# Two attention ends: odd sequences' exact scores in two banks more, normalised input turned in another bank, half of the perceptron's first layer ahead of the last weighing

## The reference

```python
# second attention layer (and, with other weights and no gate, the fifth)
qc = (_ln(x) @ cq_W) per head;  kc, vc = (cond_tokens @ ck_W, @ cv_W) per head   # 77 keys
x  = x + g_x * (softmax(qc @ kc.T / sqrt(8), masked) @ vc) @ co_W
# the perceptron behind it
xm = _ln(x) * (1 + sc_mlp) + sh_mlp
x  = x + g_mlp * (gelu(xm @ mlp_W1 + mlp_b1) @ mlp_W2 + mlp_b2)
```

## Time and profile before

| | us |
|---|---|
| median of 3 runs | 1077.26 (1077.23 to 1077.37) |
| profiled execution, its own time | 1078.58 |
| its span, first to last instruction | 1076.8 |
| TensorE busy in it | 1024.1 (95%) |
| VectorE / GpSimd / ScalarE busy | 780.5 / 681.1 / 593.2 |
| mean granted TensorE clock | 0.978 |

### The profile page before, as it was taken

One profiled execution on the slowest core, in us unless ns is written; L12 is line 12 of the kernel. 1 busy time (PEld: TensorE's weight loads), 2 busy tenths in 40 slices (PEclk: granted clock), 3 DMA queues, 4 the chain that ended last, 5 costly groups with the idle time before them and its releaser, 6 DMA issues.

```text
span 1076.8 us, 28749 instructions
## 1 busy us (share of the span) xinstructions
PE 1024.1 (95%) x11713; PEld 643.3 (60%) x11713; DVE 780.5 (72%) x1940; ACT 593.2 (55%) x842; POOL 681.1 (63%) x783
## 2 busy tenths in 40 slices
PE   7899999999998999999999699999999999999898
PEld 5345555666654776667766455665655566565476
DVE  7889888788874444777777979888888766777321
ACT  2144444577666454555444266665666667765652
POOL 6688887688974432111214689987888766788520
PEclk9699999999999999999999789999999999999999
DMA  6200000000000102000000000000000000000011
GB/s 218 112 2 3 21 12 12 23 12 22 21 12 24 39 29 101 7 6 7 7 7 18 13 7 2 2 2 2 2 2 2 2 2 2 2 2 2 2 39 40
DMA packets 9282, 22.76 MB, mean 21 GB/s; under 512 B 1392, under 2 KB 1648, under 8 KB 8768
## 3 DMA queue, kind: packets, MB, share of 16 engines
q1 hardware_dynamic: 9152, 20.94, 5.8%
HBM read 18.77 MB, written 2.15 MB: 19 GB/s over the span
## 4 chain that ended last, share of the span: by engine, by line
PE 82%; DVE 8%; issue 4%; ACT 3%; POOL 2%; DMA 0%; SPq 0%; DVEq 0%; POOLq 0%; ACTq 0%
PE weighed L674 12%; PE scores L647 11%; PE row_scores L616 8%; PE scores L861 6%; PE weighed L697 5%; PE quads L552 4%; PE scores L571 4%; DVE negmax L1171 3%; PE quads L578 3%; PE row_scores L861 3%; PE quads L563 3%; PE scores L659 3%; PE scores L687 2%; ACT p L1662 2%; PE weighed L872 2%
## 5 line engine op out<-in xcount | busy, mean ns | idle before, releaser
L1171 DVE TENSOR_REDUCE negmax<-row_scores 128x8 f32<-128x616 f32 (+1 forms) x312 | 298.9, 958 | 86.1 <-PE row_scores L616 67.4
L1662 ACT ACTIVATE p<-scores 128x1024 f32<-128x1024 f32 (+1 forms) x256 | 247.6, 1018 | 156.6 <-PE scores L659 156.3
L647 PE MATMUL scores<-qblk,work 32*77 32x512 f32 (+1 forms) x1280 | 203.7, 612 | 10.2 <-ACT p L1662 6.8
L1840 POOL TENSOR_TENSOR kblk_r<-work,pack_const 128x308 fp32r<-128x308 f32 (+1 forms) x160 | 133.6, 836 | 75.3 <-PE row_scores L616 55.4
L674 PE MATMUL weighed<-p,v 77*32 77x128 f32 (+1 forms) x5120 | 173.1, 276 | 2.5 <-DVE nat L1196 2.5
L1830 POOL TENSOR_TENSOR qblk<-work,pack_const 128x512 f32<-128x512 f32 x160 | 166.0, 1038 | 0.9 <-PE scores L647 0.9
L616 PE MATMUL row_scores<-kblk_r,qr 32*128 32x308 f32 (+1 forms) x624 | 142.3, 447 | 18.4 <-DVE negmax L1171 17.3
L674 PEld LDWEIGHTS weighed<-p,v 77*32 77x32 f32 (+1 forms) x5120 | 130.1, 109 | 37.9 <-issue 33.5
L616 PEld LDWEIGHTS row_scores<-kblk_r,qr 32*128 32x128 f32 x624 | 62.0, 187 | 120.0 <-issue 84.5
L1877 POOL TENSOR_TENSOR attn<-nat,rden 128x128 f32<-128x128 f32 x160 | 65.6, 410 | 57.8 <-DVE rden L1201 56.9
L1196 DVE STREAM_TRANSPOSE nat<-weighed 128x256 f32<-128x256 f32 x160 | 70.8, 442 | 34.2 <-PE weighed L674 33.8
(11 more groups left out here) (309 smaller groups left out, 1850.3 us busy)
## 6 DMA issues: line engine op xcount, KB each, us to landing
shared<-gates_hbm SPq DMA_DIRECT2D x24, 256.0 KB, 3.2
shared<-in_ctx_tok SPq DMA_DIRECT2D x15, 154.0 KB
pack_w_l<-in_w_l SPq DMA_DIRECT2D x1, 2058.5 KB, 11.3
x<-in_x_tok SPq DMA_DIRECT2D x8, 256.0 KB, 5.8
out_x<-x SPq DMA_DIRECT2D x8, 256.0 KB, 2.0
layers_w<-in_w_l SPq DMA_DIRECT2D x1, 1289.0 KB, 9.4
ctxT<-in_ctxT SPq DMA_DIRECT2D x1, 1232.0 KB, 9.4
layers_w<-in_w_ada SPq DMA_DIRECT2D x1, 582.0 KB, 5.1
```

Source lines behind the costliest of these rows:

```text
L647: mm = e.matmul(scores[0:nk, g, :], k_of[q % 3][at, s * nk:(s + 1) * nk], qblk[n % 2][at, :], start=layer.mask != "qk", stop=False, skip_g ...
L1171: e.tensor_reduce(negmax[q % 2][:, 2 * h:2 * h + 2, s * NJ:(s + 1) * NJ], row_banks(n, h)[:, :, 0:NJ * nk].rearrange("p g (j k) -> p g j k ...
L1662: e.activation(p[n % 2][0:nk, 8 * h:8 * h + 8, :], scores[0:nk, 2 * h:2 * h + 2, :].rearrange("p g (j q) -> p (g j) q", j=NJ), ACT.Exp, bi ...
L1840: e.tensor_tensor(kblk_r[n % 2][:, 0:NJ * nk].rearrange("p (j k) -> p j k", j=NJ), k_of[q % 3][:, s * nk:(s + 1) * nk].unsqueeze(1).to_bro ...
```

## The change

In the last five slots of each phase the exact scores of an odd sequence (59, 61, 63 and 155, 157, 159) put their second half, groups 2 and 3, in the two banks of `row_scores`, whose row maxima are all taken by then; their Exp reads it there. Even sequences stay in the four banks of `scores`. With that, `exact` in these slots waits for `exp_done >= 2n - 1`, the first half of the sequence before, and for all row maxima. `shift` is called once per half. The perceptron's norms of slots 59, 63 and 155, 159 are turned in the quads' bank (`quad_bank`), and no wait of `exact` stands behind them. `first_layer` of the first quad is split: its chunks 0 and 1 (banks 2 and 3 of `scores`) stand ahead of the last `weigh`, chunks 2 and 3 (`row_scores`) behind it. `project_out` in slots 62 and 158 drops its wait for an Exp.

```diff
+        def turned_in_quads(it):
+
+
+            return not it.family or 0 < 4 * PHASES[it.q >= 2 * NB][1] - it.slot <= 5
+
         def turned_bank(it):
-
-            return scores[:, 1, :] if it.family else quad_bank[:, :]
+            return quad_bank[:, :] if turned_in_quads(it) else scores[:, 1, :]
...
             return any(4 * lo <= n < 4 * lo + 4 for lo, _ in PHASES)
+
+        def from_end(n):
+
+            return min(4 * hi - n for _, hi in PHASES if n < 4 * hi)
+
+        def score_banks(n, h):
+
+
+            return row_scores[:, :, :] if h and n % 2 and from_end(n) <= 5 else scores[:, 2 * h:2 * h + 2, :]
...
                 layer, nk = layer_of(q), layer_of(q).nk
-                w.wait_ge(exp_done, 2 * n)
+                if from_end(n) <= 5:
+                    w.wait_ge(exp_done, 2 * n - 1)
+                    w.wait_ge(max_done, 2 * (n + from_end(n)))
+                else:
+                    w.wait_ge(exp_done, 2 * n)
                 ready, value = k_ready(q)
...
                     at = slice(TILE * g, TILE * (g + 1))
-                    mm = e.matmul(scores[0:nk, g, :], k_of[q % 3][at, s * nk:(s + 1) * nk], qblk[n % 2][at, :],
+                    mm = e.matmul(score_banks(n, g // 2)[0:nk, g % 2, :], k_of[q % 3][at, s * nk:(s + 1) * nk], qblk[n % 2][at, :],
                                   start=layer.mask != "qk", stop=False, skip_group_check=True,
...
-            def shift(n):
+            def shift(n, h):
                 q, s = divmod(n, QUAD)
...
                 w.wait_ge(act_setup, ACT_AT["select"])
-                for g in range(NG):
-                    at = slice(TILE * g, TILE * (g + 1))
-                    mm = e.matmul(scores[0:nk, g, :], select[at, s, 0:nk], nblk[q % 2][at, :], start=False, stop=True,
-                                  skip_group_check=True, tile_position=(TILE * g, 0))
-                    if g % 2:
-                        mm.then_inc(shifted, 1)
+                for i in range(2):
+                    at = slice(TILE * (2 * h + i), TILE * (2 * h + i + 1))
+                    mm = e.matmul(score_banks(n, h)[0:nk, i, :], select[at, s, 0:nk], nblk[q % 2][at, :], start=False, stop=True,
+                                  skip_group_check=True, tile_position=(TILE * (2 * h + i), 0))
+                mm.then_inc(shifted, 1)
...
-            def first_layer(phase, c, hi):
+            def first_layer(phase, c, hi, chunks=range(4)):
                 weight, in_done, act_done = (("l0_w1", mlp_in, mlp_act), ("l3_w1", ffn_in, ffn_act))[phase]
...
                 w.wait_ge(max_done, 8 * hi)
-                w.wait_ge(exp_done, 8 * hi)
+                w.wait_ge(exp_done, 8 * hi - (2 if chunks.stop == 2 else 0))
                 w.wait_ge(ln_done, NORM_OF[("l0m", "l3f")[phase], hi - NB + c].index + 1)
-                for f in range(4):
+                for f in chunks:
                     w.wait_ge(act_done, 4 * (c - 1) + f + 1)
...
                     qi, cl = divmod(t, QUAD)
-                    if t in norm_at and norm_at[t].family:
+                    if t in norm_at and not turned_in_quads(norm_at[t]):
                         w.wait_ge(ln_scaled, norm_at[t].index + 1)
...
                         w.wait_ge(raw_done, (qi + 3) % NB + 1)
-                    if t in norm_at and not norm_at[t].family:
+                    if t in norm_at and turned_in_quads(norm_at[t]):
                         w.wait_ge(ln_scaled, norm_at[t].index + 1)
...
                         turn_x(qi + 3)
-                    if t in norm_at and not norm_at[t].family:
+                    if t in norm_at and turned_in_quads(norm_at[t]):
                         turn_normed(norm_at[t])
                     if cl == 2 and qi - 2 in quads and not is_wide(t):
-                        w.wait_ge(exp_done, early)
+                        if qi >= hi:
+                            w.wait_ge(exp_done, early)
                         project_out(qi - 2)
...
                         exact(t)
-                        shift(t)
+                        shift(t, 0)
+                        shift(t, 1)
                     if is_wide(t):
...
                     else:
+                        if t == 4 * hi:
+                            first_layer(phase, 0, hi, range(2))
                         if t - 1 in jobs:
...
                         keep_busy(5, scores[:, 0, 0:128])
-                    if first_layer_at(t, hi) is not None:
-                        first_layer(phase, first_layer_at(t, hi), hi)
+                    c = first_layer_at(t, hi)
+                    if c is not None:
+                        first_layer(phase, c, hi, range(0 if c else 2, 4))
                     if second_layer_at(t, hi) is not None:
...
                 w.wait_ge(wo_read, 2 * NB - 2)
+                w.wait_ge(ln_scaled, NORM_AT[0][8 * NB - 1].index + 1)
                 w.wait_ge(fold_done, k)
...
                 e.activation(p[n % 2][0:nk, 8 * h:8 * h + 8, :],
-                             scores[0:nk, 2 * h:2 * h + 2, :].rearrange("p g (j q) -> p (g j) q", j=NJ), ACT.Exp,
+                             score_banks(n, h)[0:nk].rearrange("p g (j q) -> p (g j) q", j=NJ), ACT.Exp,
                              bias=hide, scale=HEAD_SCALE).then_inc(exp_done, 1)
```

## The result

| | before | after |
|---|---|---|
| median, us | 1077.32 (1077.23 to 1078.09, 4 runs) | 1065.82 (1064.89 to 1066.40, 4 runs) |
| profiled execution, us | 1078.58, span 1076.8 | 1065.88, span 1064.1 |

The ratio is 0.9891, with a 95% interval of 0.9876 to 0.9906: 11.5 us less. The two profiled executions are 12.7 us apart.

A forecast was written before the change was run, and what follows sets the result against it. TensorE was taken as the bound, in a relay with ScalarE at the phases' ends. Gains of 6.3 (fifth layer) + 6.8 (second) = 13.1 us, from the 1077.26 median, gave 1064.1 us; 1062 to 1069 holds about 8 in 10.

The forecast's parts named there:

- likeliest case: Whole kernel: the change works as summed, 1064.1 us, own spread 1062 to 1066, chance 0.62.
- Part 1: Slot 156: the exact scores' wait for `hat`, 0.85 us, goes because the norm is turned in the quads' bank.
- Part 2: Slots 157 and 158: exact scores wait for the first Exp half only; slots shrink from 3.32 to 2.36 us.
- Parts 3 and 4: Slot 159: exact scores start 3.0 us earlier, behind the output projection; its norm is turned 3.2 us earlier.
- Part 5: Last norm to first layer: chunks 0 and 1 ahead of `weigh` hide `hat` and `nat`; 1.5 us saved.
- Covers: Slack at the ends: 0.3 us before `weigh` waits for the second Exp half, 0.8 us before `qblk` is late.
- Part 6: First layer and projection at the ends: clock no longer falls, saving 1.65 us (fifth layer) and 1.8 us (second).
- The low stretches stay: Both ends: the clock still falls once, so 3.4 us are not gained, 1067.5 us; chance 0.14.
- Lost on the way: Second phase's start or mixture takes up the 6.8 us gained at the second layer's end: 1070.9 us; chance 0.10.
- Doesn't do what it says: Last slots: wait moves to `weigh` or `qblk`, slots stay near 3.3 us, only 6.3 us gained, 1070.9; chance 0.06.
- Slower: Clock low from slot 155 through the first layer, 19 us more, 1083 us at one end alone; chance 0.05.

The follow-up runs named there:

- experiment 2: Changed kernel with only the norms turned in the quads' bank kept; scores in four banks with full wait, first layer unsplit: 1074.35 us, ratio 0.9972.
- Experiment 5: Changed kernel, but exact scores of the last five slots wait for both halves of the Exp ahead; banks still alternate: 1070.40 us, ratio 0.9937.
- experiment 3: Changed kernel with the first layer whole behind the last weighing (no split): 1070.11 us, ratio 0.9929.
- experiment 1: Changed kernel with only the alternating score banks and half-Exp wait kept; norms turned in `scores` again, first layer unsplit: 1073.39 us, ratio 0.9964.
- experiment 4: Changed kernel with the change at the second layer's end only; `project_out` still drops its wait at both ends: 1070.64 us, ratio 0.9939.
- experiments 10 and 11: Changed kernel plus idle matmuls at the second phase's start, 58 and then 33: 1065.10 us, ratio 0.9887, and 1065.15 us, ratio 0.9892.
- 8: Kernel before, unchanged, profiled once more: 1077.21 us, one execution.
- 9: Kernel before, unchanged, profiled once more: 1077.36 us, one execution.
- experiment 12: Changed kernel with all four chunks of the first quad's first layer ahead of the last weighing: 1067.21 us, ratio 0.9907.
- 6: Kernel before plus eight idle matmuls in the hole ahead of the last weighing of each phase: 1076.84 us, ratio 0.9998.
- 7: Kernel before, unchanged, profiled once more: 1077.49 us, one execution.

## Why the prediction was right, and the term that was not

The forecast was 1064.1 and the time 1065.82, inside the range and inside the likeliest case's own 1062 to 1066. Point by point, by the prediction's numbers:

- **Part 1**, slot 156 without `hat`: a first slot of 2.98 us was forecast, 2.86 came at both ends. Alone (experiment 2) it makes this slot 0.5 to 0.6 us shorter, since a wait for the Exp stands right behind the one for `hat`.
- **Part 2**, the relay as 1.34 + half an Exp + 0.05: 2.36 and 2.45 us forecast, 2.41 to 2.47 and 2.50 to 2.55 came. ScalarE sets the second of the two slots, as said. The first, the longer one, is TensorE's own 2.25 us and the 0.2 us for which `weigh` waits for `nat`; the prediction had 0.1 us for this and took it for hidden. Experiment 5 takes only the half Exp away and the old slots return.
- **Parts 3 and 4**: 3.34 us with the projection, 3.35 came. The norm turned 3.2 and 3.6 us earlier, 3.12 and 3.58 came.
- **Part 5**, the split: 1.5 us forecast, 1.30 came (experiment 3). The 0.2 us are that a pair of chunks next to a weighing takes 1.82 us and not 1.72 (998.54 to 1000.36 and 1001.37 to 1003.19, against 1004.08 to 1005.80), and the split has two such pairs. Not forecast at all was that the split also takes 0.5 us off the next norm's wait for GpSimd at each end (0.63 against 1.13 us).
- **Covers**. `weigh` inherits the wait for the second half: no row of it; its one wait is the short one for `nat`. `qblk` of 158: no wait. The Exp of 158 was feared 0.1 to 0.2 us late through the root and isn't late at all. Exps that read banks of both kinds take 1.93 us a pair as before (991.38 to 993.31), the lower end of the bounds, as taken.
- **Part 6, the clock, was mis-sized.** It was counted as 1.65 + 1.8 us, certain. Two things are wrong with that. It is there in some executions only. The hole of 1.23 us stands at 15 ends among the profiles (eight of the kernel before, six of experiments 1 to 3, one of experiment 4), and the clock fell behind five of them: at both ends in 2 of 4 profiles of one and the same program, and at one in experiment 1. And where it is there it costs 1.2 us net, since the next norm waits for GpSimd's `xh` 0.5 us longer when the first layer is fast.

So the ends give 12.4 us against profiles with the low stretches and 5.2 + 4.8 = 10.0 against those without; the mean is 11.2, and 11.5 was measured. Term by term against that mean, by the estimate under the table: slots 6.8 forecast and 6.4 measured, split 2.9 and 3.6, clock 3.4 and 1.2. The forecast took its sum of 13.1 from one profile, which had the low stretches, and subtracted it from the median, which lay 1.3 us under that profile's own time. From its own time the same sum gives 1065.5, and 1065.88 came. That the sum fits so well there is in part luck: the profile that was read happened to have both low stretches, and the 0.5 us an end by which they are worth less is what the split, unforeseen, takes off the next norm's wait.

**The rivals.** *The low stretches stay* falls: the changed kernel has none, at either end, and experiments 3 and 5 have none either. *Lost on the way* falls by experiment 4. *Doesn't do what it says* falls by the waits: nothing moved to `qblk`, and only 0.2 us in one slot of each end to `weigh`. *Slower* falls by the stretches: the clock is 1.00 over all alternating slots. The swinging clock that goes with cycling through accumulator banks (the Trainium skill, TensorE: Matmul & The Clock Gate, section "A second HAM failure mode: psum-queue depth-cycling") is not borne out here: experiment 5 alternates with 1.0 to 1.2 us of idle time in two slots of each end at a clock of 1.00. Another section of that page, "What's actually happening", says that the chip looks at TensorE's activity in windows of its own; that would let the same hole count in one execution and not in the next, and 2 of 4 profiles of one program agree with it. No run here shows that this is the cause.

**What stays open.** Why the clock falls behind one hole and not behind the same hole in the next execution stays open. Starts and middles differ from one execution to the next by over 1 us, in code that the change doesn't touch, and (idle matmuls of experiments 10 and 11 included) over all 14 profiles they go with the mean granted clock of one stretch each:

| stretch | granted clock | profiles | length of start or middle, us |
|---|---|---|---|
| 20 to 60 us | 0.66 | changed, 8, 9, 12 | start 324.4 to 324.7 |
| | 0.74 | before, 1, 2, 3, 5, 6, 7, 11 | start 323.4 to 324.1 |
| | 0.79 | 4, 10 | start 323.0 and 323.2 |
| 590 to 630 us | 0.74 | before, 2, 4, 8, 9 | middle 641.9 to 642.8 |
| | 0.79 and more | the other nine | middle 641.2 to 641.6 |

That explains the 0.57 and 0.87 us between the two profiles of the result, as far as rows that go together can. It also agrees with experiments 10 and 11: the changed kernel's profile was at 0.79 already, and more brought nothing. The 0.3 us between 11.5 and 11.2, a median and a mean of profiles, is of the size of these differences. They also hide what the ends do: the profiles of the kernel before without low stretches had starts of 324.6 and 324.7 us, the others 323.4 and 323.8, and all four spans lie within 1.4 us. Whether the changed kernel is ever low at an end I can't say either: its own profile and those of experiments 10 and 11, which share its ends, are not.

## What to carry to other kernels

Where two engines pass the same buffers to and fro, the period is a latency plus one engine's whole job; let the next job start on the half that is free first, with the wait for its second half handed to a consumer that comes late anyway, and the period falls by half that job. Work that needs neither of the late results (here half of the next layer, into the banks that are free first) belongs into the hole in front of a late result, and no more of it than there are free banks.

A clock that is low behind a hole in one profile is no fixed cost: profile the same kernel two or three times, and look whether the next wait takes part of it back, before it goes into a sum. And subtract a sum from the time of the execution that it was read from.

## What the runs showed of the hardware

- The granted clock behind a hole of 1.2 us fell to 0.50 in some executions and stayed at 1.00 in others of the same program, at the same place. Idle time of 1.0 to 1.2 us in each of two slots, between stretches of 2.25 us of work, never brought it down: at both ends of all four profiles of the kernel before and of experiments 2, 5 and 6, and at the fifth layer's end of experiment 4.
- A pair of 128x512 float32 matmul chunks takes 1.72 us among its like and 1.82 us beside a weighing, which works on 32-column tiles of the array: 0.1 us for each change between the two. The output projection shows the same on both sides: from start to start it takes 0.89 us between full-array work (1003.19 to 1004.08), 0.99 with exact scores behind it (983.72 to 984.71) and 1.09 between a weighing and exact scores (994.71 to 995.80). The Trainium skill, TensorEngine Tiling (Array Packing), section "Key Properties", says that changing the tiling mode drains the engine; these rows agree. The first pair of experiment 12, which follows a wait and no change, takes 1.82 us too: a start out of idle time seems to cost as much.
- Idle matmuls brought a low stretch from 0.50 to 1.00 and the time did not move, with VectorE busy 5.90 of 6 us: what a clock is worth depends on who sets the pace there.
